# Attention scores over the whole array, one per unit and a unit ahead, behind the transposes

## The reference

```python
x = x + mamba_block(layernorm(x))          # Mamba-2: in-projection, conv, scan, gate, out-projection
x = x + xattn(layernorm(x), ctx, ctx, adj, mask)
x = x + ffn(layernorm(x))                  # one of 8 expert matrices per position, the same for all batches

# xattn, 16 heads of 16 channels
Q, K, V = heads(x @ Wq.T + bq), heads(ctx @ Wk.T + bk), heads(ctx @ Wv.T + bv)
scores = Q @ K.T / 4 + adj                 # (8, 16, 512, 512)
weights = softmax(where(mask == 0, -inf, scores))
out = (weights @ V) @ Wo.T + bo
```

## Time and profile before

| | us |
|---|---|
| median of 3 runs | 1268.09 (1267.8 to 1269.53) |
| the profiled execution | 1269.45 |
| its span | 1267.7 |
| TensorE matmul busy | 1141.1 |
| VectorE busy | 996.4 |
| ScalarE busy | 782.1 |
| GpSimd busy | 636.1 |

### The profile page before, as it was taken

The page is one execution under the profiler, slowest core; times in us unless marked ns, Lnnn a source line. Parts: engine busy times, 40 slices in busy tenths (PEclk is TensorE's granted clock), DMA queues, the critical chain, the costliest instruction groups (busy, mean ns, idle before and its releaser), DMA issues. The chain is left out here.

```text
span 1267.7 us, 29908 instructions
## 1 busy us (share of the span) xinstructions
PE 1141.1 (90%) x10292; PEld 788.5 (62%) x10292; DVE 996.4 (79%) x2530; ACT 782.1 (62%) x1452; POOL 636.1 (50%) x554
## 2 busy tenths in 40 slices
PE   4587999999999999999999999999999999887387
PEld 2255666666667677666766666767776676655244
DVE  5765888788879887888888887888888887755486
ACT  2224675767776677667766766767566776766242
POOL 4572466327833584446544773278144653300375
PEclk9798999999999999999999999999899999989699
DMA  6042105410432024401540053103240143020511
GB/s 206 0 117 76 51 1 146 116 32 26 113 96 85 26 68 105 122 4 42 133 129 16 26 151 99 46 26 103 75 124 2 45 98 96 25 57 19 208 78 58
DMA packets 101524, 96.52 MB, mean 76 GB/s; under 512 B 17184, under 2 KB 76832, under 8 KB 100096
## 3 DMA queue, kind: packets, MB, share of 16 engines
q1 hardware_dynamic: 92912, 76.42, 20.0%
q0 software_dynamic: 6240, 17.57, 5.9%
q10 hardware_dynamic: 2224, 0.62, 0.2%
HBM read 71.49 MB, written 27.26 MB: 78 GB/s over the span
## 5 line engine op out<-in xcount | busy, mean ns | idle before, releaser
L902 ACT ACTIVATE T<-T,nmx 128x512 f32<-128x512 f32 x512 | 368.7, 723 | 215.6 <-DVE nmx L1269 213.6
L1269 DVE CUSTOM_DVE_ANT_0 T<-ps,am 128x512 f32<-128x512 f32 x512 | 346.3, 684 | 117.0 <-PE ps L687 115.2
L695 PE MATMUL pt<-ident,T 128*128 128x128 f32 x2048 | 324.8, 283 | 15.2 <-ACT PT L893 14.4
L695 PEld LDWEIGHTS pt<-ident,T 128*128 128x128 f32 x2048 | 231.9, 142 | 121.0 <-issue 87.8
L893 ACT COPY PT<-pt 128x512 f32<-128x512 f32 x352 | 201.9, 573 | 15.8 <-PE pt L695 15.1
L1385 POOL TENSOR_TENSOR dmask<-triu,dA 128x1024 fp32r<-128x1024 f32 x64 | 132.5, 2134 | 49.7 <-DVE dA L1113 49.5
L687 PE MATMUL ps<-k_st,q_st 64*128 64x512 f32 x512 | 131.0, 504 | 22.1 <-DMA q_st<-q_d 21.6
L712 PE MATMUL po<-PT,va 128*32 128x128 f32 x4096 | 139.2, 277 | 10.4 <-issue 6.2
L1360 POOL TENSOR_TENSOR xc<-xc,ygT 128x512 f32<-128x512 f32 x90 | 119.5, 1328 | 13.4
L1423 POOL TENSOR_TENSOR rr<-se,nhalf 128x1 f32<-128x1 f32 x32 | 22.1, 690 | 207.2 <-DVE se L1199 200.2
L712 PEld LDWEIGHTS po<-PT,va 128*32 128x32 f32 x4096 | 105.4, 110 | 33.3 <-issue 32.1
(11 more groups left out here) (216 smaller groups left out, 1950.3 us busy)
## 6 DMA issues: line engine op xcount, KB each, us to landing
k_st<-k_d SPq DMA_DIRECT2D x256, 64.0 KB, 2.2
q_st<-q_d SPq DMA_DIRECT2D x256, 64.0 KB, 2.4
am<-in_mask SPq DMA_DIRECT2D x8, 1024.0 KB, 5.4
k_d<-kp SPq DMA_DIRECT2D x32, 256.0 KB, 2.7
am<-in_adj POOLq DMA_DIRECT2D x8, 1024.0 KB, 10.6
q_d<-qp SPq DMA_DIRECT2D x128, 64.0 KB, 1.6
x_in<-in_x SPq DMA_DIRECT2D x8, 512.0 KB, 4.4
ctx_in<-in_ctxT SPq DMA_DIRECT2D x8, 512.0 KB, 4.1
```

The costliest lines, as they stand in the source:

```text
L695: ins = pe.transpose(pt[u % 2][:, kt * P:(kt + 1) * P], T[:, u % RING, kt * P:(kt + 1) * P], ident[:, :])
L902: act.activation(T[:, u % RING, :], T[:, u % RING, :], ACT.Exp, bias=nmx[:, u % RING:u % RING + 1], scale=-1.0).then_inc(sems["probs"], 1)
L1269: dve.tensor_tensor_reduce(T[:, u % RING, :], ps[(a * UNITS + u) % S_BANKS][:, :], ams[a % 2][:, qt, :], -1.0, 3e38, ALU.add, ALU.min, nmx ...
```

## The change

Each head gets its own slot of 128 rows in `q_st` (`AH` in the place of `HP`), with the queries in its own half and zeros in the half of its neighbour; VectorE writes those zeros once, at the start. A score then multiplies 128 rows: the neighbour's keys meet zeros. It is one full-array matmul per unit, of the same 512 columns. In TensorE's loop the score of unit u + 1 is issued in slot u, behind the four transposes of unit u - 3 and ahead of `pv` and the stages; it was issued in pairs, units u and u + 1 at even slots, ahead of the transposes. The larger `q_st` takes its room from V: `VW` is 17, and the column tiles stay 32 apart (`VT`), so `po` is cleared once at the start. The buffers of the last stage that lay in `vas` move to `pre` and to a joint array of `x_in` and `ctx_in`, and what GpSimd waits for ahead of the load of the biases follows.

```diff
-VW = 32
+VW = 17
+VT = 32
...
-        x_in = sb("x_in", [P, C, E])
-        ctx_in = sb("ctx_in", [P, KE, S])
+        xio = sb("xio", [P, 2, C * E])
+        x_in = xio[:, 0, :].rearrange("p (c e) -> p c e", c=C)
+        ctx_in = xio[:, 1, :].rearrange("p (k s) -> p k s", k=KE)
...
-        q_st = sb("q_st", [P, 2, HP, P], F32R)
+        q_st = sb("q_st", [P, 2, AH, P], F32R)
...
-                            sp.dma_start(q_st[(4 * h + r) * AD:(4 * h + r + 1) * AD, c % 2, :, :].bitcast(F32), src[h]).then_inc(sems[f"q_in{c % 2}"], 16)
+                            sp.dma_start(q_st[(4 * h + r) * AD:(4 * h + r + 1) * AD, c % 2, :, :].rearrange("p (n h) i -> p h n i", h=2)[:, h, :, :].bitcast(F32), src[h]).then_inc(sems[f"q_in{c % 2}"], 16)
...
-                    half = slice(h % 2 * P // 2, (h % 2 + 1) * P // 2)
-                    pe.matmul(ps[(a * UNITS + u) % S_BANKS][:, :], q_st[half, qt % 2, h // 2, :], k_st[half, h // 2, :], start=True, stop=True,
-                              tile_position=(h % 2 * P // 2, 0)).then_inc(sems["score"], 1)
+                    if a == 0 and u == 0:
+                        pe.wait_ge(setup["zeros"], 4)
+                    mm(ps[(a * UNITS + u) % S_BANKS][:, :], q_st[:, qt % 2, h, :], k_st[:, h // 2, :], True, True).then_inc(sems["score"], 1)
...
+                    if a == 0 and n == 0:
+                        pe.wait_ge(setup["sums"], 1)
...
-                            ins = pe.matmul(po[VW * hh:VW * (hh + 1), g * P:(g + 1) * P], vas[a % 2][:, kt, g * HG + hh, :], PT[:, n % 2, hh, kt, :],
-                                            start=(kt == 0), stop=(kt == C - 1), tile_position=(0, VW * hh), skip_group_check=True)
+                            ins = pe.matmul(po[VT * hh:VT * hh + VW, g * P:(g + 1) * P], vas[a % 2][:, kt, g * HG + hh, :], PT[:, n % 2, hh, kt, :],
+                                            start=(kt == 0), stop=(kt == C - 1), tile_position=(0, VT * hh), skip_group_check=True)
...
                 for s_ in range(SLOTS):
-                    a, u = divmod(s_ - LEAD, UNITS)
-                    if 0 <= a < B and u % 2 == 0:
-                        score(a, u)
-                        score(a, u + 1)
                     a, v = divmod(s_ - LEAD - LAG, UNITS)
                     if 0 <= a < B:
                         turn(a, v)
+                    a, u = divmod(s_ + 1 - LEAD, UNITS)
+                    if 0 <= a < B:
+                        score(a, u)
...
+                dve.memset(po[:, :], 0.0).then_inc(setup["sums"], 1)
+                for i in range(2):
+                    for h in range(2):
+                        dve.memset(q_st[(1 - h) * P // 2:(2 - h) * P // 2, i, :, :].rearrange("p (n h) q -> p h n q", h=2)[:, h, :, :].bitcast(F32), 0.0).then_inc(setup["zeros"], 1)
...
-                pool.wait_ge(sems["pv"], at("pv", B - 1, 0))
+                pool.wait_ge(sems["conv_dve"], DC * sum(len(conv_split(b)[1]) for b in range(B)))
+                pool.wait_ge(sems["conv_pool"], DC * sum(len(conv_split(b)[0]) for b in range(B)))
```

More of the change, by code:

```diff
@@ L282, in build @@
         x_f = [kp[:, :, :, :].rearrange("p o k s -> p (o k s)").bitcast(F32), xnr[:, :, :, :].rearrange("p o c e -> p (o c e)"),
-               xc[:, :, :].rearrange("p c s -> p (c s)")[:, 0:ROW], vas[1][:, :, :, :].rearrange("p c h v -> p (c h v)"),
+               xc[:, :, :].rearrange("p c s -> p (c s)")[:, 0:ROW], xio[:, :, :].rearrange("p i n -> p (i n)"),
                T[:, :, :].rearrange("p r s -> p (r s)")]
         seg_w = [ap[:, :, :].rearrange("p c s -> p (c s)").rearrange("p (j k e) -> p j k e", j=P // SEG, k=KE) for ap in ams]
-        b_f = vas[0][:, :, :, :].rearrange("p c h v -> p (c h v)")[:, 0:BLOCKS * E].rearrange("p (k e) -> p k e", e=E)
+        b_f = pre[:, :, :].rearrange("p n s -> p (n s)")[:, 0:BLOCKS * E].rearrange("p (k e) -> p k e", e=E)
         n_f, t_f = zt, xnT
@@ L301, in build @@
         m_read = [sem(f"m_read{k}") for k in range(M_BANKS)]
-        setup = {n: sem(f"setup_{n}") for n in ("act", "dve", "pool", "scaled", "pad")}
+        setup = {n: sem(f"setup_{n}") for n in ("act", "dve", "pool", "scaled", "pad", "zeros", "sums")}
         PER = dict(
```

## The result

The changed kernel takes 1280.76 us in the median (1272.02 to 1284.30), the kernel before beside it on the same chip 1269.92 (1267.53 to 1271.85): a ratio of 1.0073, 95% interval 1.0051 to 1.0094, some 9 us slower. Forecast were 1265, between 1251 and 1274.

A forecast was written before the change was run, and what follows sets the result against it. TensorE's order was taken as the bound. Terms -0.5 (first batch), -3.6 (six batches), -0.3 (start, other query waits), -3.3 (tail), +4.5 (clock) sum to -3.2; off the median 1268.09 that gives 1264.9, said as 1265, range 1251 to 1274.

The forecast's parts named there:

- The bound and the price of a score: TensorE's order bounds batches; a whole-array score takes 0.235 us, saving TensorE 14 us (10 to 17), 1.7 per batch.
- rival (c): TensorE's whole-array scores: weight loads are not hidden, 56 us less the 14, so 1310 us; chance 0.05.
- The growth of the border's wait: At batch borders TensorE's wait for queries grows from 1.7 to about 3.2 us; a batch gains 0.6.
- rival (a): At borders the wait doesn't grow, VectorE reaching the split of q about 1.5 us sooner: 1251 us; chance 0.23.
- I take no new one: At a batch's other three query tiles: no new wait for queries (0 to 0.3 us each).
- The clock: Behind border waits: two or three more falls of TensorE's granted clock, 4.5 us (0 to 12), 1.7 us a fall.
- Rival (b): Behind each border the clock makes it slower, over 0.2% from six more falls; ten more give 1277 us; chance 0.20.
- The tail: In the window from 1146.40, scores ahead cut VectorE's waits: 3.3 us off (0 to 4.5); four units in 5 us, not 6.
- The memsets: VectorE's new memsets at the start, under its wait for x, cost 0 to 2.0 us; taken as 0.

The follow-up runs named there:

- With queries on time: Kernel before and changed kernel, both with q split two slots sooner (first, third tile), projection and split sooner in last batch: 1257.16 and 1242.83 us.
- the falls filled away: Changed kernel plus unread identity transposes while TensorE waits for queries, at six borders and the last batch's third and fourth tiles: 1262.68 us, ratio 0.9948.
- its waits filled: Kernel before plus unread transposes in its query waits, 12 at six borders, 28 and 18 in the last batch: 1265.55 us, ratio 0.9982.
- q_sooner_after: Changed kernel with VectorE's split of q two slots sooner for first and third query tiles, three for the fourth: 1262.84 us, ratio 0.9951.

## Why the prediction was wrong

**The bound and the price of a score: right.** 0.235 forecast, 0.25 read at the border above; no load that is not hidden, so rival (c) is out, and the product with V kept its 1.00. What that saves is right in the total only. With queries on time 14.3 us reach the end, where 14 of TensorE and 3.3 of the tail were forecast, but not as 1.7 a batch: the six batches between give 5.4 together, 0.9 each, the first one 4.4 and the last one 3.0. That the total comes near 14 is luck. Why the batches between give half of 1.7 no run shows.

**The growth of the border's wait: right in size.** 1.7 to 3.2 forecast; 3.47 at the border shown, 2.5 on the mean of seven, against 1.3 before; two of the seven are over 3, not five. The chain did not start sooner, so rival (a) is out. But more than the saving was lost: a batch was to gain 0.6, and with the falls filled away the six between take 819.6 us from first score to first score, 0.9 more than before and 1.0 more than the kernel before with its waits filled (818.6).

**"I take no new one": wrong.** The step on the other three tiles of a batch looked only at how many waits there had been. The same product with V was taken from ahead of their first scores, and it had hidden queries that came up to 1.1 us late without showing a wait. Of the 15.4 us by which the waits grew, the sum let the saving cancel seven times 1.5, 10.5; the other 4.9 are not in it. The place is off by more: the borders took 8.5, the other tiles and the last batch 6.6.

**The clock: the step that decided.** Two or three more falls, 4.5 us, were taken. At the lower level are 20 us more than before (40.8 against about 20), six more falls of 3.4. Filling took 37.4 us of low clock away (3.4 are left) and gave 11.6 us between the two profiled executions, 18 between the medians: 1.1 to 1.6 for a fall, and about 0.5 in the kernel before, so the price of 1.7 was high, and the count was low. From border to border the 11.6 us between sum and profile lie here. The first batch is 2.6 shorter, where 0.5 was forecast. The six between are 9.6 longer, where the sum with its 4.5 for the clock had 0.9. From the last border's first score to the last score it is 1.6 longer, where 3.6 shorter was forecast. Filling takes 8.8 of these 9.6 away again, and 4.2 of the last stretch. The medians say it too: with the falls filled away the kernel is 6.6 us below before, where the sum without its clock term said 7.7. Part of this agreement is luck, as filling takes 2.3 us from before as well, which leaves 4.3 between the two kernels with their waits filled, and the new waits were not in the sum. Rival (b), chance 0.20, "from six more on the kernel is slower", is what happened, and it deserved more: the text itself said that five borders would wait over 3 us, and the earlier trace rows had falls behind two waits hardly longer than the one without (1.76 and 1.81 against 1.67 us). Those rows were reason to count a fall at each long wait.

**The tail: right in kind, hidden.** From the last border's first score to the last score it was 108.6 before and 110.2 after, with 17 us at the lower clock against 10, and 3.1 us more of waiting for queries. With queries on time it gives 3.0, where 3.3 and 0.3 were forecast. Four units of the tail take 5.4 us instead of 5.8 on the mean, not 5 instead of 6.

**The memsets: a little over nothing.** VectorE's five new ones end at 6.4 us, past the arrival of x, and its first statistics start at 6.33 instead of 5.45; the first score is 0.4 later. The range of 0 to 2.0 held, the 0 did not.

Open stays what decides whether a given wait is followed by a fall. In the changed kernel's profile, border waits of 2.6, 2.7, 3.1 and 3.5 us are, those of 1.4, 2.1 and 2.2 are not, yet two of 1.0 and 1.1 ahead of a third tile are, each with another wait of 0.6 us less than 2 us ahead of it; before, falls followed waits of 1.76 and 1.81, and none one of 2.02. Executions of the changed kernel differ with it: the longest, 1284.3, had a mean granted clock of 0.959, the shortest, 1272.0, 0.968, and 0.009 of 1276 us is 11.5; but one of 1275.8 had 0.968 too.

## What to carry to other kernels

Before an instruction that waits for a transfer is moved ahead of work, read how late the transfer is behind that work: the work is its cover, also where the trace of before shows no wait. On an engine that is 90% busy, as here, a wait costs more than itself when the clock falls behind it; cost each long wait with a fall, or keep the engine at work through it, and see first whether the chain that feeds it can start a slot or two sooner. A saving that seems to vanish may be waiting for exactly that: here the same change is worth 0.7% of loss or 1.1% of gain.

## What was not expected of the hardware

Two matmuls of 64 rows in the two halves of the array take together as long as one alone (0.43 and 0.42 us). A tensor operation of VectorE with two inputs of 128x256 took 1.52 us instead of 0.43 beside an addition of GpSimd: in q_sooner_after in all 12 cases that had one beside them, and in none of the other 20. The Trainium skill, page "GPSIMD Engine Reference", section "1. Specifications", says that the two engines share their interfaces to SBUF and contend when VectorE's instruction has two inputs there. These rows agree.
